# All four transpositions and the scores of a tile in the slot behind its projections

## The reference

```python
for i in range(DEPTH):            # DEPTH = 6
    x = attn_layer(shift_tokens(x), Wqkv[i], q_scale[i], k_scale[i], Wo[i]) + x
    x = ffn_layer(shift_tokens(x), ln_g[i], ln_b[i], W1[i], b1[i], W2[i], b2[i]) + x
# attn_layer: q, k, v = split(x @ Wqkv), 16 heads of 64
#   q = rotary(l2norm(q) * qs); k = rotary(l2norm(k) * ksc)
#   per window of 32 tokens: softmax(8 * q k^T over this window and the one before, masked) @ v
#   out @ Wo
# ffn_layer: layer norm, h = xn @ W1 + b1 (128 -> 682), a * gelu(gate) @ W2 + b2
```

## Time and profile before

| | |
|---|---|
| three runs | 3481.99, 3482.67 (median), 3487.38 us |
| the profiled execution | 3483.61 us, of it the span 3481.8 us |
| PE busy | 3337.9 us, 96% of the span |
| DVE, ACT, POOL busy | 82%, 70%, 67% |
| granted TensorE clock | 0.985 on average over the span |

### The profile page before, as it was taken

How to read it: one execution, slowest core, us unless ns; L and a number is a source line. 1 busy time by engine, 2 the same in 40 slices (tenths; PEclk the granted TensorE clock), 3 DMA queues, 4 the chain that set the end, 5 groups by cost and what they waited for, 6 DMA issues and landing times.

```text
span 3481.8 us, 123144 instructions
## 1 busy us (share of the span) xinstructions
PE 3337.9 (96%) x51660; PEld 1871.0 (54%) x51660; DVE 2858.4 (82%) x6052; ACT 2433.7 (70%) x4133; POOL 2342.3 (67%) x2188
## 2 busy tenths in 40 slices
PE   6999999999999999999788999999999999999996
PEld 3555555555555555555354555555555555555553
DVE  7888888888888888886468888888888888888883
ACT  3677777777777777777425777777777777777775
POOL 5777777777776777775137777777777777677771
PEclk8999999999999999999899999999999999999999
DMA  2001001001001001000100000000010000000000
GB/s 84 12 15 46 12 14 49 12 14 48 12 15 48 12 14 36 10 13 20 39 1 24 14 24 22 17 24 22 12 29 22 12 28 23 12 28 10 12 5 13
DMA packets 49223, 76.64 MB, mean 22 GB/s; under 512 B 7072, under 2 KB 37024, under 8 KB 47136
## 3 DMA queue, kind: packets, MB, share of 16 engines
q1 hardware_dynamic: 48672, 68.76, 6.3%
HBM read 61.39 MB, written 7.34 MB: 20 GB/s over the span
## 4 chain that ended last, share of the span: by engine, by line
PE 51%; POOL 22%; issue 15%; DVE 10%; ACT 1%; POOLq 0%; DMA 0%; SPq 0%; DVEq 0%; ACTq 0%
PE QA L835 10%; PE VS L899 10%; POOL QN L345 8%; POOL QN L352 8%; PE TB L923 6%; PE TB L854 5%; PE VS L949 4%; PE FB L986 4%; POOL Z L361 3%; PE TB L878 3%; DVE T L607 3%; DVE T L602 3%; PE FB L977 3%; PE FB L978 2%; POOL TAB L337 2%
## 5 line engine op out<-in xcount | busy, mean ns | idle before, releaser
L345 POOL TENSOR_TENSOR QN<-T 128x512 f32<-128x512 f32 x768 | 979.4, 1275 | 570.3 <-DVE T L607 551.7
L352 POOL TENSOR_TENSOR QN<-QN,RR 128x512 f32<-128x512 f32 x768 | 792.6, 1042 | 154.4 <-DVE RR L628 154.4
L835 PE MATMUL QA<-WQ,Y 128*128 128x512 f32 x1536 | 753.5, 603 | 23.0 <-DVE T L607 14.7
L899 PE MATMUL VS<-MW,Y 128*32 128x512 f32 x6144 | 738.5, 598 | 6.7 <-DVE Z L694 6.4
L602 DVE TENSOR_TENSOR T<-QA,TAB 128x512 f32<-128x512 f32 x768 | 525.4, 684 | 187.1 <-ACT SQ L452 178.2
L472 ACT ACTIVATE V<-VS 128x512 f32<-128x512 f32 x768 | 455.2, 601 | 251.4 <-PE VS L899 251.2
L923 PEld LDWEIGHTS TB<-CST,QN 128*128 128x128 f32 x3072 | 354.3, 141 | 491.8 <-issue 278.1
L452 ACT ACTIVATE SQ<-QA 128x512 f32<-128x512 f32 x768 | 441.4, 595 | 193.6 <-PE QA L835 182.2
L607 DVE TENSOR_TENSOR T<-QA,TAB 128x256 f32<-128x256 f32 x1536 | 572.4, 414 | 0.0
L361 POOL TENSOR_TENSOR Z<-Z,RC 128x512 f32<-128x512 f32 x384 | 394.4, 1048 | 237.2 <-DVE RC L664 235.1
L923 PE MATMUL TB<-CST,QN 128*128 128x128 f32 x3072 | 483.9, 280 | 34.4 <-DVE Y L634 20.9
(11 more groups left out here) (167 smaller groups left out, 4106.5 us busy)
## 6 DMA issues: line engine op xcount, KB each, us to landing
TAB<-in_tables SPq DMA_DIRECT2D x192, 128.0 KB, 2.1
WQ<-in_w_qk SPq DMA_DIRECT2D x48, 256.0 KB, 3.2
m_dram<-MW SPq DMA_DIRECT2D x6, 1024.0 KB, 5.6
MW<-m_dram SPq DMA_DIRECT2D x6, 1024.0 KB, 5.7
W1R<-in_w SPq DMA_DIRECT2D x12, 341.0 KB, 3.0
WS<-in_w_vt SPq DMA_DIRECT2D x6, 512.0 KB, 5.8
WS<-in_w_out SPq DMA_DIRECT2D x6, 512.0 KB, 5.3
W<-in_w SPq DMA_DIRECT2D x12, 192.0 KB, 2.9
```

Source lines behind the costliest of these rows:

```text
L345: po.tensor_tensor(QN[:, n % 2, k, :], T1[:, k, :], T2[:, k, :], ALU.add).then_inc(s_add, 1)
L352: po.tensor_tensor(heads(QN[:, m % 2, k, :]), heads(QN[:, m % 2, k, :]), RR[:, m % 2, 8 * k:8 * k + 8].unsqueeze(2).to_broadcast([P, 8, DH ...
L835: mm(QA[:, k % 2, :], Y[:, j * P:(j + 1) * P], WQ[:, k, :], start=True, stop=True).then_inc(s_qk, 1)
L899: last = mm(VS[32 * q:32 * q + 32, w % 2, :], Y[:, a:a + WIN], MW[:, l % 2, q, :], start=True, stop=True, tile_position=(0, 32 * q), skip_ ...
```

## The change

Pieces 2 and 3 of tile t are transposed, and its scores computed, in slot t+1, where only pieces 0 to 2 were transposed before; everything behind the scores moves up by one slot with them (lags 3, 4, 5 become 2, 3, 4; the feed-forward kinds begin at slots 7 to 10 and so fall on c % 4 = 3, 0, 1, 2 for A, B, C, D). A stack has 103 slots.

Inside a slot PE's order changes: piece 2's transposition stands between `project_qk(2)` and `project_qk(3)`, piece 3's and the mask directly behind `project_qk(3)`, and the feed-forward matmuls of kinds A and D, which stood ahead of them, stand between the mask and the scores. On ACT piece 2's copy stands between squares 2 and 3, and no longer behind the gelu. No arithmetic, tile, transfer or buffer is added or removed. Piece 3's transposition now waits for the copy of piece 0 of its own tile; piece 2's waits, as before, for the copy of piece 1 of its own tile.

The core of the diff (PE and ACT; the rest moves lags and counts of waits by one):

```diff
-LAST = TILES + 8
+LAST = TILES + 7
...
                 if live(c, 0, it):
                     square(2)
+                if live(c, 1, it):
+                    qk_out(1, 2)
+                if live(c, 0, it):
                     square(3)
-                if live(c, 2, it):
-                    qk_out(2, 3)
+                if live(c, 1, it):
+                    qk_out(1, 3)
...
                     ac.preload_act_table_set("natural_log_exp_and_others")
-                if live(c, 1, it):
-                    qk_out(1, 2)
                 if live(c, 0, it):
                     ac.wait_ge(s_rm, by_tile(1, n, it, 1))
...
                     elif k == 2:
                         pe.wait_ge(s_te, by_tile(3, m, it, 2))
                     else:
-                        if edge:
-                            after(pe, s_pe, 2, n - 4, 1, it, s)
-                            after(pe, s_te3, 1, n - 3, 0, it, s)
-                        after(pe, s_te, 3, n - 1, 0, it, s)
+                        pe.wait_ge(s_te, by_tile(3, m, it, 1))
...
                 def scores():
-                    m = n - 2
+                    m = n - 1
                     j = m % 4
                     if j == 0 and m % TILES:
                         pe.wait_ge(s_kp, by_tile(1, m // 4, None) if it is None else it * 4 + m // 4)
+                    pe.wait_ge(s_te, by_tile(3, m, it, 3))
                     pe.wait_ge(s_te3, by_tile(1, m, it, 1))
...
                     project_qk(2)
                 if up2_g is not None:
                     ffn_down(0)
+                if live(c, 1, it):
+                    qk_transpose(1, 2)
                 if live(c, 0, it):
                     project_qk(3)
+                if live(c, 1, it):
+                    qk_transpose(1, 3)
+                    mask_scores()
                 if up2_g is not None:
                     ffn_down(1)
                 if cen_g is not None:
                     ffn_centre()
                 if up2_g is not None:
                     ffn_down(2)
...
-                if live(c, 2, it):
-                    qk_transpose(2, 3)
-                    mask_scores()
-                if live(c, 1, it):
-                    qk_transpose(1, 2)
                 if up0_g is not None:
                     ffn_up(up0_g, 0)
                 if up1_g is not None:
                     ffn_up(up1_g, 1)
+                if live(c, 1, it):
+                    scores()
                 if live(c, 2, it):
-                    scores()
-                if live(c, 3, it):
-                    p_transpose(3, 0)
+                    p_transpose(2, 0)
```

More of the change, by code:

```diff
@@ L200, in fold_piece @@
         def fold_piece(c, s):
-            if s or c % 4 or not 4 <= c < 4 + 4 * CH // 2 * (DEPTH - 1):
+            if s or c % 4 != 3 or c >= TPL * (DEPTH - 1):
                 return None
-            return (c - 4) // TPL + 1, (c - 4) // 4 % 4
+            return c // TPL + 1, c // 4 % 4
         def all_slots(engine, slot, s):
@@ L387, in slot @@
                     rot_add(2)
-                if live(c, 2, it) and (c - 2) % 4 == 3:
+                if live(c, 1, it) and (c - 1) % 4 == 3:
                     last_keys()
@@ L446, in slot @@
                 n = s * TILES + c
-                cen_g, up0_g, up1_g, up2_g = (group_of(c, first, it) for first in (8, 9, 10, 11))
+                cen_g, up0_g, up1_g, up2_g = (group_of(c, first, it) for first in (7, 8, 9, 10))
                 def square(k):
@@ L541, in slot @@
                         .then_inc(s_re, 1)
[L542 to L545, removed]
+                if live(c, 2, it):
+                    p_out(2, 0)
+                if (c - 6) % TPL == 0 and (it is not None or c < TILES):
+                    l = (c - 6) // TPL
                     ac.wait_ge(s_wf, by_layer(32, s * DEPTH + l, it, 32))
@@ L708, in slot @@
                     ins.then_inc(s_y, 1)
-                if (c - 7) % TPL == 0 and (it is not None or c < TILES):
-                    l = (c - 7) // TPL
+                if (c - 6) % TPL == 0 and (it is not None or c < TILES):
+                    l = (c - 6) // TPL
                     ve.wait_ge(s_y, by_group(1, s * GROUPS + l * NG, it, NG))
@@ L841, in attend @@
                     if edge:
-                        after(pe, s_res, 1, n - 6, 0, it, s)
+                        after(pe, s_res, 1, n - 5, 0, it, s)
                     after(pe, s_te, 3, n - 2, 2, it, s)
@@ L892, in project_v @@
                         if edge:
-                            after(pe, s_ve, 4, n - 5, 2 + w, it, s)
-                        after(pe, s_z, 1, n - 3, 0, it, s)
+                            after(pe, s_ve, 4, n - 4, 2 + w, it, s)
+                        after(pe, s_z, 1, n - 2, 0, it, s)
                     else:
@@ L908, in qk_transpose @@
                             after(pe, s_te, 3, n - 2, 0, it, s)
-                            after(pe, s_te3, 1, n - 3, 0, it, s)
-                        after(pe, s_pe, 2, n - 4, 1, it, s)
+                            after(pe, s_te3, 1, n - 2, 0, it, s)
+                        after(pe, s_pe, 2, n - 3, 1, it, s)
                     elif k == 1:
@@ L913, in qk_transpose @@
                             after(pe, s_te, 3, n - 2, 2, it, s)
-                        after(pe, s_res, 1, n - 5, 0, it, s)
+                        after(pe, s_res, 1, n - 4, 0, it, s)
                     elif k == 2:
@@ L927, in mask_scores @@
                 def mask_scores():
-                    m = n - 2
+                    m = n - 1
                     if edge:
-                        after(pe, s_z, 1, n - 3, 0, it, s)
-                    after(pe, s_ve, 4, n - 4, 3, it, s)
+                        after(pe, s_z, 1, n - 2, 0, it, s)
+                    after(pe, s_ve, 4, n - 3, 3, it, s)
                     for e in range(2):
```

75 lines of the change are left out of this document (38 added, 37 removed).

## The result

The changed kernel takes 3491.24 us (median of 20 runs, 3483.16 to 3503.9) against 3482.33 of the kernel before (20 runs, 3477.93 to 3489.39): ratio 1.0024, 95% interval 1.0016 to 1.0031. It is slower by 0.24% where 0.65% faster was forecast. The profiled run took 3493.56 us.

The account below looks back on a forecast made before the run. PE's work sets the floor, with 0.95 us a period lost to a chain that begins with ACT's order. Middle -8.8 and ends -13.8 give -22.6 us: forecast 3460 us, 0.65% faster, range 3437 to 3480.

Parts of the forecast that it names:

- the head of the change's parts: All engines: total work stays the same, no instruction added or removed, each transfer issued from the same place of its slot.
- the slower one: Rival: piece 2's transposition waits long for piece 1's copy; with a 0.60 us stall, 3526 us; chance 0.08.
- the wait for piece 1's copy: Piece 2's transposition on PE, kinds A, B and C: a stall of 0.09 us, with the restart 0.10.
- the prediction's sum: Whole kernel: middle and ends together -22.6 us against the profiled execution's 3483.6.
- Point 1 and 2, the middle: Periods of four slots: LT earlier, piece 2 waiting for piece 1's copy; -0.20 us each, 44 times, -8.8 us.
- the named wait in kind C: Piece 1's transposition on PE waits for DVE's residual: 44 times, 20.9 us in all, 0.48 each.
- the 0.40 a period: Kind C's gain: 0.50 us from LT coming earlier, less 0.10 as B's stall delays gelu.
- Point 3, the ends: Stack's ends, one slot fewer: -11.99 + 2.59 + 2.0 + 0.5 = -6.9 us per stack, twice: -13.8 us.
- One wait the prediction held to be covered: Scores wait for piece 3's copy: about 1.3 us of cover against 0.2 of latency and 0.6 of copy.
- More than the named wait goes: Rival: all of kind C's 0.95 us of waiting a period may go, 3436 us; chance 0.12.
- nothing in the middle is won: Rival: later gelu in B leaves C unchanged, 13 us of stalls take the ends' gain, 3482 us; chance 0.14.
- The table load: Rival: gelu's table load in B and C has a hidden 1.28 us drain, +74 us, 3557 us; chance 0.03.

Follow-up runs that it names:

- run 1: The changed kernel without the second wait of the scores (for piece 2's copy); 3455.35 us, ratio 0.9933 to the kernel before.
- Run 5: run 1 with piece 2's transposition behind the fourth projection and its ACT copy behind the fourth square; 3441.77 us, ratio 0.9884 to the kernel before.
- Run 4: The kernel before with one line moved on ACT, piece 2's copy ahead of the gelus; 3470.03 us, ratio 0.9965.
- runs 9 to 12: Keys' wait moved before the third projection in Run 5, run 8, run 1 plus a far-off met wait, and the kernel before: 3435.16, 3451.5, 3449.78, 3473.39 us.
- run 8: The changed kernel with the second wait of the scores moved ahead of the mask's two matmuls; 3472.64 us, ratio 0.9967 to the kernel before.
- run 2: The kernel before with the same wait for piece 2's copy added ahead of the scores; 3548.97 us, ratio 1.0188.
- run 3: The changed kernel with 127 more, already met waits at the start of PE's program; 3496.17 us, ratio 1.005 to the kernel before.

## Why the prediction was wrong

**The step that failed** stands at the head of the change's parts: "PE's, DVE's, ACT's, POOL's and the DMA's total work stays the same: no instruction is added". The diff adds a wait to `scores()`. I asked of it only whether what it waits for is there in time, and found it covered. It is covered, and it costs 36 us all the same (run 1), by standing as an instruction, one more in 146 tiles, right ahead of 256 others that TensorE takes in 1.4 us. No rival had this place: the slower one, with 8 in 100, laid the loss on the wait for piece 1's copy, which measures 0.08 (one projection and the wait are 1055.51 - 1054.57 = 0.94, a projection alone 0.86), where 0.09 was forecast. Without the added wait the forecast holds: run 1 is 25.4 us faster than before, the prediction's sum was 22.6. The middle came out as it was worked out; at the ends there is some luck in it, as will be seen.

**Point 1 and 2, the middle: -0.20 us a period forecast.** The squares of ScalarE give it: the first of tile 12 and the first of tile 92 stand 80 slots apart, 20 periods. For stack 1, before:

```profile
L452 ACT ACTIVATE SQ<-QA x2: 597/597/597, 1996.4 to 1997.3; 128x512 f32<-128x512 f32 x2
...
L452 ACT ACTIVATE SQ<-QA x2: 597/597/597, 3329.6 to 3330.4; 128x512 f32<-128x512 f32 x2
```

and in run 1:

```profile
L452 ACT ACTIVATE SQ<-QA x2: 578/584/591, 1981.4 to 1981.9; 128x512 f32<-128x512 f32 x2
...
L452 ACT ACTIVATE SQ<-QA x2: 582/586/590, 3308.7 to 3309.1; 128x512 f32<-128x512 f32 x2
```

1333.2 us become 1327.3; in stack 0, in the same way, 1343.3 become 1337.9. Together 11.3 us in 40 periods, -0.28 each; some 2.5 of it are fewer stops in the scores of these tiles (8.8 and 6.2 us, what their scores take over the undisturbed 1.48), which leaves -0.22. The change after all has both parts of the term: the named wait in kind C falls from 20.9 us to 17.4 in the waits of run 1, 0.40 a time, and piece 2 waits. Run 5 prices the latter: with two projections ahead of it three kinds of slot are each 0.11 us shorter (medians from square to square), against 0.10 forecast. Run 4 alone is 0.07 short of the 0.40 a period: from tile 12 to 92 it gains 14.4 us in 40 periods, 0.36, of which some 1.1 us are stops.

**Point 3, the ends: -13.8 forecast, -18 measured.** Run 1's span is 3481.8 - 3452.2 = 29.6 us shorter, 11.3 of it in the middle. From the last tile's first square to the copy of its output 62.6 us (stack 0) and 61.4 (stack 1) became 52.2 in both; the tiles ahead of it take 2.1 and 1.8 less, and the first twelve 3.8 and 1.1 more, since the slot that went was shorter than the one that now falls within their count. That is -8.7 and -9.9 a stack against -6.9. 2.6 us of it are stops in the scores that the kernel before had there. The granted clock may be the rest, a term that the prediction's sum doesn't have: from a stack's first square to that of tile 12 the kernel before is at 1.2 GHz for 23.7 and 19.9 us, run 1 for 11.7 and 9.7. No run tells what that is worth, nor why. One wait the prediction held to be covered: in slots without the FFN's matmuls as cover the scores wait for piece 3's copy, 10 times, 3.5 us in all (run 1's waits), all in a stack's first slots.

**The rivals.** More than the named wait goes, and nothing in the middle is won: neither; the term came as worked out. The table load: the Trainium skill's further 1.38 us of drain for a switch (ScalarE: Activation LUTs, What ACT_TABLE_LOAD costs) doesn't show after either. Behind a load, 1044.14 + 1.28 = 1045.42, and LT starts at 1045.43; ahead of it gelu ends at 1043.43 + 0.69 = 1044.12, and the load starts at 1044.14.

**What is shown and what is argued.** Shown: a separate wait right ahead of the scores makes them stop, in whichever kernel it stands, though it is met every time; moved ahead by a projection it does so hardly any more (0.3 to 2.0 us in runs 9 to 12). Moved ahead by the mask and a pair of matmuls (run 8) the change's own wait leaves 3 stops outside the tiles with the keys' wait, where the changed kernel has 18.

## What to carry to other kernels

Count the instructions in the densest stretch of an engine, and look at what stands right ahead of them: a second wait there is an instruction, and its cost isn't in what it waits for. Put all but one of the waits ahead of a longer instruction, or drop those that an in-order engine already implies. When the steady slots look as forecast and the total does not, list the idle time that no engine ends ("<- issue"), and compare it with that of before; and compare the granted clock, which can fall behind a stop.

## What was not expected of the hardware

TensorE ran dry of instructions in a kernel that is 96% busy: 41.4 us of stops, up to 2.4 us each (the 42.6 without the 1.2 at L1118, which every run has), where 256 small loads and matmuls in 1.4 us use up a 16 KB packet and the next starts late; TensorE went on 2.3 us after the packet's start in the one shown, and 2.2 to 3.2 us after it in all 163. The queue moves only 6.73 MB in 3492 us, so I take this for latency and not for want of bandwidth. Behind some stops the granted clock fell to 1.2 GHz, which in run 2 came to some 27 us beside 53 in its rows of stops. And 127 met waits in a row, two to an instruction, took 7.0 us at the start (run 3), 0.11 an instruction: a wait is cheap by itself, and dear by its place.
